# Eight full expert tiles taken from the first half of the tokens, the second half routed inside the expert loop

## The chip, the core and the metric

The kernel runs on one core of a Trainium2 chip. The metric is the device time of one execution in microseconds (us); the tables give the median of three runs. A profiled execution gives the rows that are quoted. The core's engines work side by side and meet only at semaphores: PE (TensorE, matrix products into PSUM), DVE (VectorE), ACT (ScalarE), POOL (GpSimd, which also issues gathers and scatters), and SP (SyncE, which issues most transfers here).

## The reference

One decoder layer over 2 x 1024 tokens of width 256, followed by a mixture of eight experts:

```python
x = _layernorm(x + attn(x))           # running sums of exp(keys) over the tokens
x = _layernorm(x + xattn(x, ctx))     # 16 heads, 77 context rows
# ffn:
logits = flat @ router_w.T + router_b
topk_vals, topk_idx = jax.lax.top_k(logits, 2)
topk_w = jax.nn.softmax(topk_vals, axis=-1)
for e in range(8):
    cw = jnp.sum(jnp.where(topk_idx == e, topk_w, 0.0), axis=-1)
    y = jax.nn.gelu(flat @ w1[e].T + b1[e], approximate=False)     # 256 -> 1024
    y = y @ w2[e].T + b2[e]                                        # 1024 -> 256
    out = out + y * cw[:, None]
out = _layernorm(out + hidden, ln_w, ln_b)
x = _layernorm(x + out)
```

Each token needs only its two chosen experts, so the kernel sorts the 4096 pairs of token and expert by expert and computes 128 pairs at a time.

## The kernel before

**Attention.** The 2048 tokens are 16 tiles of 128 (`TILES`), four to a chunk. After a start of its own, the cross attention runs in 64 steps (`attention_step(H)`, four steps to a token tile, each step four heads). The other stages of the layer for later tokens, and the norms, router logits and routing for earlier tokens, are hung on these steps by tables (`FIRST_STEPS`, `logits_step`, `RANKS_STEP`, `MARK_STEPS`). Every engine runs its own copy of the step loop, in the order written.

**Routing.** `SETS` splits the token tiles into 8, 4 and 4. For each set DVE finds the two best experts (`first_choice`, `second_choice`), PE counts with triangular matrices how many earlier tokens chose the same expert (`ranks`), DVE turns the ranks into places (`ranked`, `place`), and for each of the 2 x tiles pairs it writes two 128 x 128 indicator matrices (`mark`, L1211 and L1212), whose product on PE (`mark_pairs`, L1578) adds the token numbers into a table of 128 places by tile columns. Each expert owns 16 columns of places. Because the experts' tile counts are known only after the last set, DVE then makes the map (which expert and which column each of the 39 tiles has, L1269 to L1273), POOL turns it into integers (`map_tiles`), copies a tile's column of tokens and gathers the token rows (`load_tile`, L705 and L707). The first set is routed inside attention; the second partly and the third wholly after it.

**Expert loop.** 39 tiles (`SLOT_TILES`) of 128 pairs. On PE, tile t: `up(t)` (L1638, 32 products into `psum_a` or `psum_b`), `turn_rows(t+1)` (L1624, transposes of the gathered rows), `down(t-1)` (L1650, into `psum_v` or `psum_c`). ACT copies the transposed rows (`turned_rows`, L918), applies Gelu (`hidden`, L929) and prepares the weighed bias (`weighed_bias`, L941). DVE reads the gathered row's weight and row numbers (`indices`, L1294 to L1298), weighs the output (`weigh_output`, L1306), adds the input and the other expert's result if that came earlier (`sum_row`, L1317), and does the two norms (`inner_norm` L1325, `outer_norm` L1333). POOL does the powers for the norms (L723), gathers the earlier result of the same token from `weighed_outputs` (`load_base`, L714), gathers the rows of a tile five ahead, and scatters finished rows (L727). SP loads each tile's `w1` (1 MB, ring of three, `load_w1`) and stores the weighed outputs (`store_yw`).

**What ties them.** `up(t)` waits for the transposed rows, for `w1` and for Gelu of tile t-2; `down(t)` for Gelu of its tile and for `weigh_output(t-2)`; `weighed_bias(t)` for `sum_row(t-2)`; `load_base(t)` for the store of tile t-1; `load_w1(t)` for Gelu of tile t-3.

## Time and profile before

| | us |
|---|---|
| median of three runs (lowest, highest) | 557.19 (555.75, 559.47) |
| profiled execution, its time | 557.52 |
| its span in the trace | 555.7 |
| PE busy | 497.9 (90%), x3293 |
| DVE busy | 398.5 (72%), x1230 |
| ACT busy | 251.9 (45%), x838 |
| POOL busy | 259.9 (47%), x374 |

The span is cut into 40 equal slices of 13.9 us. Each digit is the busy share of a slice in tenths; PEclk is the granted clock of TensorE in tenths of full speed.

```profile
PE   6678999989999999418999999999999999999970
...
DVE  5768878676859986851568777776777778767744
ACT  3355667555765566103344344444443344344410
POOL 4543132221312300343367666675676767666643
PEclk9899999989999999857999999999999999999995
```

The chain that ended last, by engine:

```profile
PE 80%; DVE 10%; issue 2%; POOL 2%; DMA 2%; ACT 1%; SPq 1%; POOLq 0%; ACTq 0%; DVEq 0%
```

### The profile page before, as it was taken

To read this page: it belongs to the slowest core of one execution; us is meant where nothing else is said; L and a number is where in the kernel's file an instruction comes from. 1 tells how busy PE (TensorE), PEld (TensorE's weight loads), DVE (VectorE), ACT (ScalarE), POOL (GpSimd) and SP (SyncE) were. 2 spreads that over 40 slices of the span, in tenths; PEclk is the share of its full clock that TensorE was granted. 3 is DMA by queue.
4 is the path that set the end of the run, shared out by engine and by line. 5 is a ranking of instruction groups with operands and counts; after the bars stand their busy time and mean duration, and the time that the engine had idled before them with its cause. 6 is when DMAs were issued, how large, how long until landed. Compare 5 with 4: busy or idle time off the path is not lost.

```text
span 555.7 us, 10856 instructions
## 1 busy us (share of the span) xinstructions
PE 497.9 (90%) x3293; PEld 448.3 (81%) x3293; DVE 398.5 (72%) x1230; ACT 251.9 (45%) x838; POOL 259.9 (47%) x374
## 2 busy tenths in 40 slices
PE   6678999989999999418999999999999999999970
PEld 6567888878887877307999999999999999999960
DVE  5768878676859986851568777776777778767744
ACT  3355667555765566103344344444443344344410
POOL 4543132221312300343367666675676767666643
PEclk9899999989999999857999999999999999999995
DMA  7119991000000050027566555556566666666310
GB/s 226 13 38 335 338 321 50 11 9 11 11 9 11 11 120 21 24 90 280 189 202 211 197 203 196 194 203 216 209 220 216 222 211 221 214 217 211 97 46 16
DMA packets 43873, 81.14 MB, mean 146 GB/s; under 512 B 10768, under 2 KB 35610, under 8 KB 38696
## 3 DMA queue, kind: packets, MB, share of 16 engines
q1 hardware_dynamic: 36567, 67.36, 35.9%
q0 software_dynamic: 5616, 12.82, 7.6%
q8 instruction: 28, 0.46, 0.3%
q10 hardware_dynamic: 1632, 0.27, 0.3%
q14 instruction: 30, 0.24, 0.1%
HBM read 65.64 MB, written 17.63 MB: 150 GB/s over the span
## 4 chain that ended last, share of the span: by engine, by line
PE 80%; DVE 10%; issue 2%; POOL 2%; DMA 2%; ACT 1%; SPq 1%; POOLq 0%; ACTq 0%; DVEq 0%
PE psum_a L1638 13%; PE psum_b L1638 12%; PE psum_c L1650 12%; PE psum_v L1650 12%; PE psum_b L1377 7%; PE psum_v L1510 5%; PE psum_a L1476 5%; PE psum_m L1528 2%; PE psum_m L1377 2%; PE psum_c L1497 2%; PE psum_m L1624 2%; PE psum_a L1479 1%; DMA second_buffers<-in_x 1%; PE psum_c L1492 1%; PE psum_b L1384 1%
## 5 line engine op out<-in xcount | busy, mean ns | idle before, releaser
L929 ACT ACTIVATE front_then_w_ring<-psum_a,front_then_w_ring 128x128 f32<-128x128 f32 x160 | 45.7, 369 | 81.8 <-PE psum_a L1638 78.9
L1638 PEld LDWEIGHTS psum_a<-front_then_w_ring 128*128 128x128 f32 x640 | 76.8, 197 | 2.0 <-issue 1.0
L1638 PE MATMUL psum_a<-front_then_w_ring 128*128 128x128 f32 x640 | 77.0, 280 | 0.6 <-ACT front_then_w_ring L918 0.6
L929 ACT ACTIVATE front_then_w_ring<-psum_b,front_then_w_ring 128x128 f32<-128x128 f32 x152 | 43.5, 369 | 74.3 <-PE psum_b L1638 72.0
L823 ACT ACTIVATE work<-psum_a,score_max 128x77 f32<-128x77 f32 x256 | 62.4, 335 | 29.8 <-DVE score_max L1081 29.7
L1638 PEld LDWEIGHTS psum_b<-front_then_w_ring 128*128 128x128 f32 x608 | 70.8, 192 | 2.5 <-issue 1.6
L1650 PE MATMUL psum_v<-expert_w,front_then_w_ring 128*128 x320 | 72.4, 379 | 0.0
L1638 PE MATMUL psum_b<-front_then_w_ring 128*128 128x128 f32 x608 | 71.0, 275 | 1.4 <-ACT front_then_w_ring L918 1.4
L1650 PE MATMUL psum_c<-expert_w,front_then_w_ring 128*128 x304 | 68.8, 379 | 0.0
L1650 PEld LDWEIGHTS psum_v<-expert_w,front_then_w_ring 128*128 128x128 f32 x320 | 59.3, 190 | 7.3
L723 POOL TENSOR_TENSOR routing<-routing,minus_half 128x2 f32<-128x2 f32 x40 | 29.2, 729 | 74.0 <-DVE routing L1313 72.8
L1650 PEld LDWEIGHTS psum_c<-expert_w,front_then_w_ring 128*128 128x128 f32 x304 | 56.3, 190 | 6.9
L714 POOL DMA_INDIRECT work<-weighed_outputs,routing x39 | 46.4, 1190 | 16.8 <-issue 11.9
L1377 PE MATMUL psum_b<-front_then_w_ring,front_weights_then_tail 128*128 128x256 f32 (+1 forms) x216 | 48.6, 370 | 1.9 <-ACT front_then_w_ring L801 1.8
L1325 DVE SCALAR_TENSOR_TENSOR work<-work,routing,front_weights_then_tail 128x256 f32<-128x256 f32 x39 | 19.3, 496 | 37.0 <-POOL routing L723 37.0
L727 POOL DMA_INDIRECT out<-work,routing x39 | 40.2, 1030 | 12.1 <-issue 6.1
L1510 PEld LDWEIGHTS psum_v<-front_weights_then_tail,work 128*128 128x128 f32 x320 | 40.6, 192 | 5.1 <-issue 4.7
L1377 PEld LDWEIGHTS psum_b<-front_then_w_ring,front_weights_then_tail 128*128 128x128 f32 x216 | 37.7, 190 | 8.0 <-ACT front_then_w_ring L801 2.7
L707 POOL DMA_INDIRECT front_then_w_ring<-token_rows,routing x39 | 38.3, 983 | 11.1 <-POOL routing L705 10.8
L1510 PE MATMUL psum_v<-front_weights_then_tail,work 128*128 128x136 f32 x320 | 43.1, 282 | 0.0
L544 POOL TENSOR_TENSOR ln_rstd<-ln_veps,minus_half 128x2 f32<-128x2 f32 (+1 forms) x18 | 12.5, 696 | 59.3 <-DVE ln_veps L970 59.3
L567 POOL TENSOR_TENSOR routing<-routing,minus_half 128x1 f32<-128x1 f32 x16 | 10.4, 647 | 63.5 <-DVE routing L1046 63.5
(214 smaller groups left out, 927.0 us busy)
## 6 DMA issues: line engine op xcount, KB each, us to landing
front_then_w_ring<-in_w1b SPq DMA_DIRECT2D x39, 1028.0 KB
expert_w<-in_w SPq DMA_DIRECT2D x8, 1024.0 KB, 10.7
weighed_outputs<-routing SPq DMA_DIRECT2D x1, 4992.0 KB, 16.8
weighed_outputs<-work SPq DMA_DIRECT2D x39, 128.0 KB, 2.0
token_rows<-front_then_w_ring SPq DMA_DIRECT2D x16, 128.0 KB, 1.9
second_buffers<-in_x SPq DMA_DIRECT2D x4, 256.0 KB, 4.8
front_weights_then_tail<-in_b SPq DMA_DIRECT2D x1, 1024.0 KB, 8.3
front_then_w_ring<-in_x SPq DMA_DIRECT2D x3, 256.0 KB, 4.6
```

The lines of the kernel that those rows point to most:

```text
L707: pool.indirect_dma_start(xt[t % ROWS], None, rows_dram, bass.IndirectOffsetOnAxis(load_of[:, t % ROWS:t % ROWS + 1], 0)).then_inc(xt_in[t ...
L714: pool.indirect_dma_start(base[t % 3], None, yw_dram, bass.IndirectOffsetOnAxis(row_idx[:, t % IDX, 0:1], 0)).then_inc(base_in[t % 3], 16)
L723: pool.tensor_tensor(rstd[:, t % 4], veps[:, t % 2], mhalf[:, 0:2], ALU.pow).then_inc(rstd_out, 1)
L727: pool.indirect_dma_start(out, bass.IndirectOffsetOnAxis(row_idx[:, t % IDX, 1:2], 0), u_rows[t % 3], None, bounds_check=T - 1, oob_is_err ...
L823: last = act.activation(prob[:, u % RING_U, at_k:at_k + SC], pa[:, H % 2, g * SC:(g + 1) * SC], ACT.Exp, bias=smax[:, j % 2, head:head + 1])
L929: last = act.activation(hidT[t % 2][:, c, :], src[:, n, q * P:(q + 1) * P], ACT.Gelu, bias=bias[:, c:c + 1])
L1325: row(dve.scalar_tensor_tensor(u, base[t % 3], out_mv[:, t % 2, 0:1], lnw_s, ALU.subtract, ALU.mult))
L1377: last = pe.matmul(dst[:, c, :], w[:, k, c * P:(c + 1) * P], src[:, k, :], start=(k == 0), stop=(k == KD - 1))
L1476: pe.matmul(dst, qT[it % 2][:, half, j * P:(j + 1) * P], kbd[:, it // CPB, half, g * HG:(g + 1) * HG, :].rearrange("p h k -> p (h k)"), st ...
L1510: last = pe.matmul(pv[:, half * width:(half + 1) * width], probT[:, u % RING_U, c, :], vblk[:, t // (CPB * CT), half, c, :], start=(c == 0 ...
L1638: last = pe.matmul(dst[:, n, q * P:(q + 1) * P], w1[:, k, c * P:(c + 1) * P], xtT[t % 2][:, k, :], start=(k == 0), stop=(k == KD - 1))
L1650: last = pe.matmul(y_psum(t), hidT[t % 2][:, c, :], w2_v[:, bass.ds(e, 1), c, :].rearrange("p a d -> p (a d)"), start=(c == 0), stop=(c == ...
```

## The change

`SETS` becomes two halves of eight token tiles. Once the first half is routed, inside attention, a first map takes the first eight full tiles of 128 pairs that it holds (`first_map`, `FIRST = 8`); they are expert tiles 0 to 7, and they need no later token. Their pairs keep their places; pairs of the first half beyond them get 32768 added to their slot (`LATER`), so that of a token's two results the one computed later is known. The second half is routed after attention, while PE works on the first expert tiles: DVE does it between its work for tiles 0, 1 and 2, and a second map (`rest_map`, `later_map`) covers the other 31. PE starts tile 0 directly behind the last weighing of values, in halves (`up(t, n)`) put between the last tiles' projection, transposes and logits. The products for the first half's marks stand at step 56 of attention, those for the second half's behind `up(3)`.

Weighed outputs are stored by their slot (128 columns of 128 rows, `YW_COLS`), no longer by tile number, so DVE's correction of row numbers (three instructions of `indices`) goes, SP reads a column number before each store, and the array to be zeroed grows from 39 to 128 columns: 16 transfers of 1 MB, two behind each `store_x2` of tiles 2 to 9. The second half's token rows are zeroed too (`clear_rows`). The exponential of the routing moves from ACT to POOL, as a power. SP loads `w1` of tiles 0 to 2 behind `store_x2(10)`, inside attention, and POOL gathers the rows of tiles 0 to 3 in steps 58 and 62.

At the start of the kernel, the moments of x pieces 3 and 4 and the mask are moved behind the first key sums, and the warm-up products on PE go from 14 to 9. `slot(8)` and `slot(11)` change places.

```diff
-SETS = ((0, 2 * CT), (2 * CT, CT), (3 * CT, CT))
+SETS = ((0, TILES // 2), (TILES // 2, TILES // 2))
+LATER = 32768.0
-RANKS_STEP = (CHUNKS - 1) * STEPS + 3
+RANKS_STEP = (CHUNKS - 1) * STEPS + 1
...
+            def store_yw(t):
+                sp.wait_ge(yw_ready, t + 1)
+                col = nc.values_load(store_col_of[0:1, t:t + 1], engines=[mybir.EngineType.SP], min_val=0, max_val=YW_COLS - 1,
+                                     skip_runtime_bounds_check_because="the map keeps it below the number of columns")
+                sp.dma_start(yw_cols[bass.ds(col, 1)].rearrange("a p d -> p (a d)"), yw[t % 3]).then_inc(yw_out[t % 3], 16)
...
                 store_x2(t)
+                if t < 10:
+                    clear_yw(2 * t - 4)
+                    clear_yw(2 * t - 3)
+                if t == 10:
+                    store_ext(0)
+                    for n in range(RING3):
+                        load_w1(n)
...
             def mark_pairs(n):
-                    last = pe.matmul(pc[:, 0, 0:P], *marks_of(n, i), start=(done + i == 0), stop=(done + i == PAIRS - 1))
+                    last = pe.matmul(table_psum(n), *marks_of(n, i), start=(i == 0), stop=(i == SET_PAIRS[n] - 1))
...
-            for t in range(SLOT_TILES):
-                up(t)
+            for t in range(2, SLOT_TILES):
+                up(t, 0)
+                up(t, 1)
+                if t == 3:
+                    pe.wait_ge(placed, 3 * LAST + 1)
+                    mark_pairs(LAST)
                 if t + 1 < SLOT_TILES:
                     turn_rows(t + 1)
-                if t >= 1:
-                    down(t - 1)
+                if t - 1 == FIRST:
+                    pe.wait_ge(map_ready, 2 * MAPS)
+                down(t - 1)
```

The order on DVE behind attention is written out:

```diff
+            route_logits(TILES - 1)
+            first_choice(LAST)
+            second_choice(LAST)
+            indices(2)
+            weigh_output(0)
+            add_input(0)
+            rest_map()
+            ranked(LAST)
+            place(LAST)
+            for i in range(SET_PAIRS[LAST] // 2):
+                mark(LAST, i)
+            dve.wait_ge(ln_in, 2 * 16)
+            indices(3)
+            weigh_output(1)
+            add_input(1)
+            sum_row(0)
+            for i in range(SET_PAIRS[LAST] // 2, SET_PAIRS[LAST]):
+                mark(LAST, i)
+            later_map()
+            row(inner_norm(0))
+            sum_row(1)
+            dve.memset(token_of[:, P:COLS], 0.0)
+            dve.wait_ge(pos_mm, LAST + 1)
+            dve.tensor_tensor(token_of[:, 0:P], table_psum(LAST), first_token_of, ALU.add).then_inc(table_ready, 1)
+            for t in range(2, SLOT_TILES):
```

On PE, behind the last weighing of values (L1510), before the change. L1443 transposes a normed tile, L1564 to L1570 are rank counts, L1452 logits, L1528 the output projection, L1578 products of marks:

```order
L1443 MATMUL psum_b<-identity,front_then_w_ring 128x128 x2
L1520 MATMUL psum_m<-identity,work 128x128 x2
L1564 MATMUL psum_v<-routing 128x32
...
L1452 MATMUL psum_a<-front_weights_then_tail,work 128x8 x2
L1528 MATMUL psum_m<-front_weights_then_tail,work 128x256 x2
L1443 MATMUL psum_b<-identity,front_then_w_ring 128x128 x2
L1452 MATMUL psum_a<-front_weights_then_tail,work 128x8 x2
L1578 MATMUL psum_c<-front_then_w_ring 128x128 x16
...
L1578 MATMUL psum_c<-front_then_w_ring 128x128 x8
L1624 MATMUL psum_m<-identity,front_then_w_ring 128x128 x2
L1638 MATMUL psum_a<-front_then_w_ring 128x128 x16
```

The same place after it (L1677 is `turn_rows`, L1690 `up`, L1702 `down`):

```order
L1514 MATMUL psum_c<-identity,front_then_w_ring 128x128 x2
L1677 MATMUL psum_c<-identity,front_then_w_ring 128x128 x2
L1690 MATMUL psum_a<-front_then_w_ring 128x128 x8
L1589 MATMUL psum_m<-identity,work 128x128 x2
L1521 MATMUL psum_c<-front_weights_then_tail,work 128x8 x2
L1690 MATMUL psum_a<-front_then_w_ring 128x128 x8
L1677 MATMUL psum_c<-identity,front_then_w_ring 128x128 x2
L1597 MATMUL psum_m<-front_weights_then_tail,work 128x256 x2
L1514 MATMUL psum_c<-identity,front_then_w_ring 128x128 x2
L1690 MATMUL psum_b<-front_then_w_ring 128x128 x8
L1521 MATMUL psum_c<-front_weights_then_tail,work 128x8 x2
```

The first expert products moved ahead of everything but one transpose, and the marks moved away. On DVE, where the second half's places are made, after the change (L1344 is `weigh_output`, L1339 `add_input`, L1274 to L1282 `rest_map`, L1295 and L1296 marks):

```order
L1213 TENSOR_TENSOR routing<-routing 128x64
...
L1344 SCALAR_TENSOR_TENSOR work<-psum_v,routing,work 128x256
L1339 TENSOR_TENSOR work<-work,front_then_w_ring 128x256
L1274 TENSOR_SCALAR routing<-psum_c 128x8
...
L1224 TENSOR_TENSOR routing<-psum_c,routing 128x64
L1230 TENSOR_TENSOR routing<-routing 128x64
...
L1245 CAST routing<-routing 128x4x8
L1295 TENSOR_SCALAR second_buffers<-routing 128x128
L1296 TENSOR_SCALAR second_buffers<-routing 128x128
```

Tile 0's output is weighed between the choice and the places, and eight more pairs of marks stand behind tile 1's output and tile 0's sum.

## Rows read from the trace of the kernel before

**Rows 1.** window: length, busy PE PEld DVE ACT POOL, PEclk, DMA share, GB/s.
```profile
223.00:251.00 28.00, 9.07 (x70) 5.75 (x68) 19.85 (x98) 3.02 (x6) 11.67 (x29) 0.67 0.20 61
```

**Rows 2.** timeline of PE: start, duration, line, output and inputs, count.
```profile
221.73 1.32 PE L1510 MATMUL psum_v<-front_weights_then_tail,work 128*128 128x136 f32 x10
...
225.02 1.13 PE L1528 MATMUL psum_m<-front_weights_then_tail,work 128*128 128x256 f32 x4
...
251.60 6.09 PE L1638 MATMUL psum_a<-front_then_w_ring 128*128 128x128 f32 x32 [0.62 <-ACT front_then_w_ring L918]
...
534.46 3.62 PE L1650 MATMUL psum_v<-expert_w,front_then_w_ring 128*128 x16
```

**Rows 3.** timeline of PE in the settled expert loop.
```profile
397.02 3.73 PE L1638 MATMUL psum_a<-front_then_w_ring 128*128 128x128 f32 x32
...
400.59 0.38 PE L1624 MATMUL psum_m<-identity,front_then_w_ring 128*128 128x128 f32 x2
...
404.26 3.73 PE L1638 MATMUL psum_b<-front_then_w_ring 128*128 128x128 f32 x32
```

**Rows 4.** timeline of ACT between attention and the first tile.
```profile
235.54 1.28 ACT L944 ACT_TABLE_LOAD   x1
...
251.08 0.38 ACT L918 ACTIVATE front_then_w_ring<-psum_m 128x256 f32<-128x256 f32 x1 [14.25 <-PE psum_m L1624]
```

**Rows 5.** timeline of DVE, choice of experts for eight token tiles.
```profile
177.31 0.22 DVE L1149 TENSOR_REDUCE routing<-logits 128x8 f32<-128x64 f32 x1
...
178.60 0.23 DVE L1161 SCALAR_TENSOR_TENSOR routing<-routing,logits 128x64 f32<-128x64 f32 x1
```

**Rows 6.** timeline of DVE, placing eight token tiles, and marks.
```profile
190.93 0.22 DVE L1194 TENSOR_TENSOR routing<-routing 128x64 f32<-128x64 f32 x1
...
192.67 0.18 DVE L1203 CAST routing<-routing 128x32 f32<-128x32 int32 x1
...
198.20 0.28 DVE L1211 TENSOR_SCALAR front_then_w_ring<-routing 128x128 f16<-128x128 f32 x1
...
198.65 0.28 DVE L1211 TENSOR_SCALAR front_then_w_ring<-routing 128x128 f16<-128x128 f32 x1
```

**Rows 7.** timeline of DVE, last reduction of the tile map.
```profile
243.92 0.74 DVE L1273 TENSOR_REDUCE routing<-routing 128x80 f32<-128x560 f32 x1
```

**Rows 8.** timeline of DVE in the settled expert loop.
```profile
403.93 0.48 DVE L1325 SCALAR_TENSOR_TENSOR work<-work,routing,front_weights_then_tail 128x256 f32<-128x256 f32 x1 [0.85 <-POOL routing L723]
...
406.32 0.15 DVE L1294 COPY routing<-front_then_w_ring 128x1 f32 x1
...
407.55 0.47 DVE L1306 SCALAR_TENSOR_TENSOR work<-psum_c,routing,work 128x256 f32<-128x256 f32 x1
...
410.66 0.48 DVE L1325 SCALAR_TENSOR_TENSOR work<-work,routing,front_weights_then_tail 128x256 f32<-128x256 f32 x1 [0.85 <-POOL routing L723]
```

**Rows 9.** timeline of PE, then windows right behind it, columns as in 1.
```profile
117.96 0.44 PE L1492 MATMUL psum_c<-identity,work 128*128 128x128 f32 x2 [1.42 <-ACT work L823]
...
120.00:122.00 2.00, 2.00 (x11) 2.00 (x11) 1.97 (x4) 1.37 (x6) 1.27 (x1) 0.50 0.00 0
122.00:124.00 2.00, 2.00 (x10) 1.77 (x9) 2.00 (x4) 1.53 (x7) 0.73 (x1) 0.68 0.00 0
```

**Rows 10.** timeline of DVE and of SP's queue, first expert number to load.
```profile
237.25 0.15 DVE L1264 CAST routing<-routing 128x1 int32<-128x1 f32 x1
...
238.12 0.36 SPq L499 DMA_DIRECT2D front_then_w_ring<-in_w1b  x1
```

**Rows 11.** timeline of ACT and DVE near the start.
```profile
12.69 0.63 ACT L796 ACTIVATE front_then_w_ring<-psum_m,bka 128x128 f32<-128x128 f32 x2 [1.31 <-PE psum_m L1377]
...
15.08 0.85 DVE L995 TENSOR_TENSOR_SCAN front_then_w_ring<-one,carry,front_then_w_ring 128x128 f32<-128x128 f32 x2
```

**Rows 12.** timeline of PE, a late wait in attention.
```profile
218.26 0.44 PE L1492 MATMUL psum_c<-identity,work 128*128 128x128 f32 x2 [0.95 <-ACT work L823]
```

**Rows 13.** DMA issues: output and input, queue, count, size, us to landing.
```profile
weighed_outputs<-routing SPq DMA_DIRECT2D x1, 4992.0 KB, 16.8
```

More of the change, by code:

```diff
@@ L314, in decoder_layer @@
         slot_hl = tmp(TOPK, TILES)
+        later, low_i, low = tmp(TILES, E), tmp(TILES, dt=I32), tmp(TILES)
         higher = tmp(TILES, E)
@@ L590, in _ @@
             block_owners()
-            for p in range(2, 5):
-                input_rsqrt(p)
+            input_rsqrt(2)
             pool.wait_ge(made, MADE)
@@ L665, in rows_of_choice, with map_tiles, first_rows_ready, load_tile @@
                 pool.tensor_scalar(ext[:, ts, :, 2], higher[:, ts], float(NOWHERE), None, ALU.add).then_inc(ext_ready, 1)
+            def map_tiles(n):
+                ts = slice(0, FIRST) if n == 0 else slice(FIRST, FIRST + XS_TILES)
+                nt = FIRST if n == 0 else XS_TILES
+                pool.wait_ge(counted, n + 1)
+                pool.tensor_copy(expert_of[:, ts], passed[:, 0, 0:nt]).then_inc(map_ready, 1)
+                pool.tensor_copy(col_of[:, ts], colf[:, 0, 0:nt]).then_inc(map_ready, 1)
+                pool.tensor_copy(store_col_of[:, ts], colf[:, 1, 0:nt]).then_inc(map_ready, 1)
+                pool.wait_ge(map_ready, (n + 1) * MAPS)
+            def first_rows_ready():
+                pool.wait_ge(table_ready, 1)
+                for j in range(2):
+                    pool.wait_ge(x2_out[j], TILES // 4 * 16)
+                pool.wait_ge(rows_clear, 2 * 16)
+                pool.wait_ge(ext_out, 16)
+                pool.wait_ge(row0_out, 3 * 16)
+            def load_tile(t):
+                if t == FIRST:
+                    pool.wait_ge(table_ready, 2)
+                    for j in range(2):
+                        pool.wait_ge(x2_out[j], TILES // 2 * 16)
+                    pool.wait_ge(ext_out, 2 * 16)
+                col = nc.values_load(col_of[0:1, t:t + 1], engines=[mybir.EngineType.Pool], min_val=0, max_val=(P if t < FIRST else COLS) - 1,
+                                     skip_runtime_bounds_check_because="a tile's column is below the number of columns")
+                if t >= ROWS:
+                    pool.wait_ge(xl_ready, t - ROWS + 1)
+                    pool.wait_ge(var_ready, t - ROWS + 1)
+                pool.tensor_copy(load_of[:, t % ROWS:t % ROWS + 1], (first_token_of if t < FIRST else token_of)[:, bass.ds(col, 1)]).then_inc(load_ready, 1)
+                pool.wait_ge(load_ready, t + 1)
+                pool.indirect_dma_start(xt[t % ROWS], None, rows_dram,
+                                        bass.IndirectOffsetOnAxis(load_of[:, t % ROWS:t % ROWS + 1], 0)).then_inc(xt_in[t % ROWS], 16)
             for H in range(CHUNKS * STEPS):
@@ L924, in hidden @@
                     act.wait_ge(y_mm, t - 1)
[L925 to L931 removed]
+                act.wait_ge(h_mm, 2 * t + n + 1)
+                for c in range(n * KF // 2, (n + 1) * KF // 2):
+                    q = c - n * KF // 2
+                    last = act.activation(hidT[t % 2][:, c, :], src[:, n, q * P:(q + 1) * P], ACT.Gelu,
+                                          bias=bias[:, c:c + 1])
+                last.then_inc(hT_made, 1)
             def weighed_bias(t):
@@ L1194, in place @@
                 then(dve.tensor_tensor(slots[:, ts], slots[:, ts], both[:, ts], ALU.mult))
+                if n == 0:
+                    then(dve.tensor_tensor(later[:, ts], slots[:, ts], over_e(threshold, nt), ALU.is_ge))
+                    then(dve.scalar_tensor_tensor(slots[:, ts], later[:, ts], LATER, slots[:, ts], ALU.mult, ALU.add))
                 then(dve.tensor_reduce(slot_hl[:, 0, ts], slots[:, ts], AX.X, ALU.max))
```

462 lines of the change are left out of this document (228 added, 234 removed).

## Prediction

> **What bounds the kernel now.** I read the engine shares and the 40 slices first: PE is busy 90% of the span, and its row has one hole, in the 17th and 18th slice. The chain that ended last is 80% PE, and no other engine is above 10% of it. The windows show the hole: from 223 to 251 us PE is busy 9.07 of 28 us and DVE 19.85, at a mean granted clock of 0.67 [rows 1]. The timelines then give its parts. PE ends the last weighing of values at 221.73 + 1.32 = 223.05, the first `up` starts at 251.60, and the last `down` ends at 534.46 + 3.62 = 538.08 [rows 2]. Inside the loop an `up` starts every 404.26 - 397.02 = 7.24 us, 3.57 of them products of `up` [rows 3], and PE does not pause. So 39 tiles are 39 x 7.24 = 282.4 us of PE, and of the 315.0 us from 223.05 to 538.08, 32.6 are not expert work. The remaining 17.6 us are the tail. In the hole, DVE works through a serial chain: second set's places and marks, third set's choice, places and marks, map; after it come a gather, a transpose and a copy.
>
> **The change, part by part.** I count PE from the end of the last weighing of values (0) and let each engine wait where the code says.
>
> *PE before tile 2.* A transpose of the normed tile and the rows of tile 0 end at 0.4. ACT copies one (0.38), loads the Gelu table (1.28) and copies the other (0.38) [rows 4]; before, the table load lay in the hole. With 0.15 for two handovers `up(0,0)` starts at 2.4, a wait of about 2.0. The small groups that stay (three transposes, one turn of heads, three logits, one projection, the rank counts) are each no longer than the projection's 1.13 [rows 2]. By their passes I take 3.2 us in all; they can't be above the 9.07 that PE was busy in the hole. Two short waits, 0.6 for the last normed tile and 0.55 for the copy of tile 2's rows, are added. This puts the logits of the last tile at 13.0, the end of `down(0)` at 16.5, `up(2)` from 17.5 to 21.1, the end of `down(1)` at 24.8, and the end of `up(3)` at 28.4. There PE must have the sixteenth pair of marks.
>
> *DVE until then.* The choice for eight tiles costs (178.60 - 177.31)/5 = 0.258 per step [rows 5]; eleven steps and two unchained ones are 3.1, so it ends at 16.3. Tile 2's indices, and weighing and input of tile 0, are 1.3: 17.6. `rest_map` has six chained steps of 0.2 and three free ones of 0.1: 19.1. Ranks 0.26, places 192.67 + 0.18 - 190.93 = 1.92 and 0.2 for the two added instructions: 21.5. A pair of marks is 198.65 - 198.20 = 0.45 [rows 6]; eight are 3.6: 25.1. Tile 1's output and tile 0's sum are 2.4: 27.5. Eight more pairs: 31.1, and the last product ends at 31.5. PE waits 3.1 us. It is this wait, for DVE's marks, that takes the place of the old one.
>
> *PE's sum.* 282.4 + 3.2 + (2.0 + 0.6 + 0.55 + 3.1) = 291.9 in place of 315.0: **-23.1 us**.
>
> *After the marks.* The second map has 32 columns; its reduction over 560 elements took 0.74 before [rows 7], and it costs 1.8 in all. Two norms and a sum put the token table at about 36.4, and tile 2's output is weighed at 40, while `down(2)` ended at 35.2: DVE is 5 us late. `down(4)` is the first to ask for it, at 46. When DVE was behind, one round took 410.66 - 403.93 = 6.73 us, 407.55 - 406.32 = 1.23 of it `indices` [rows 8]. Three of its instructions go, which leaves about 0.3, so a round is 5.8 and DVE gains 1.4 on each tile of 7.24. The lag is gone after four tiles and PE does not see it. The table is wanted by tile 8's gather, which POOL issues three tiles later. This part costs 0 as long as DVE's round stays below 7.24; if it did not, the surplus would be paid on every tile.
>
> *The clock.* Behind a wait of 1.42 us that came after thin activity, the granted clock was 0.50 and 0.68 for two windows of 2 us; that is 2 x 0.50 + 2 x 0.32 = 1.6 us lost [rows 9]. There are two idle places now, 2.0 and 3.1 us. Bounds are 0 and 3.2; I take **+1.5**, one such fall. The Trainium skill ("TensorE: Matmul & The Clock Gate", What's actually happening) says that the throttled state is the default and that activity releases it. By this rule both idle places could end at half speed, and the sum would have 3.2 where mine has 1.5.
>
> *DVE beside POOL.* The second half's weights (two powers of eight columns) run on POOL during the places and marks. The instructions of `indices` in rows 8 lie beside POOL's gathers. I add **+0.6**, between 0 and 3, to the wait for marks, as a fifth of the 3 us of places and choice.
>
> *The store's register.* Each store of weighed outputs now reads a column number after its wait. The nearest rows: DVE finishes the first expert's number at 237.25 + 0.15, and SP's load that needs it issues at 238.12 [rows 10], 0.7 us with the read. In the loop it is hidden in DVE's waiting rounds; in the tail it is on the path once. Bounds 0 and 0.7; **+0.5**.
>
> *Attention.* At the start ACT ends the first exponentials at 12.69 + 0.63 = 13.3, but DVE begins to sum at 15.08, since moments and mask stand ahead [rows 11]. Moved behind, they bring up to 1.75; I take -1.7, since the rest of the start follows from this sum. Late in attention, DVE gets some 15 more short instructions at steps 49 and 50 (3.3 us at 0.2 to 0.26 each) and loses 13 of the middle set's choice at steps 60 and 61. The second has a wait of PE of 0.95 behind it [rows 12], which goes. The first comes in one block, between maxima for which ACT and PE wait, and the products of the first half's marks come in. I take +1.3, between -1 and +3.5. Together **-0.4**. A wrong guess here moves everything behind it one for one. The transfers that are moved into attention (zero fill, `w1` of three tiles, biases) are covered by it, see the rivals.
>
> *Sum.* -23.1 + 1.5 + 0.6 + 0.5 - 0.4 = -20.9 us against the profiled execution's 557.52 (span 555.7 and 1.8 around it), which is 0.33 above the median. So 557.19 - 20.9 = **536.3 us**.
>
> **The rivals.**
>
> *The marks come later (16 in 100).* The chain on DVE between last logits and last mark has some 70 instructions and passes through PE once. If each handover or POOL's use of the same memory adds a quarter to its 18 us, PE waits 4.5 more, and with both falls of the clock 6.2: 542.5. For it: `indices` took 1.23 us for five instructions of one column [rows 8]. Against it: the marks of rows 6 are taken in the crowded part of attention. The Trainium skill ("GPSIMD Engine Reference", Key points) says that POOL shares its SBUF interfaces with VectorE and contends with its two-port modes; by this rule the marks would stretch while POOL computes the weights.
>
> *More is won (12 in 100).* The clock does not fall and the late block in attention hides: 536.3 - 1.5 - 1.5 - 1 = 532.
>
> *The zero fill comes too late (3 in 100), the other side.* SP's queue must carry 18 MB of zeros ahead of tile 0's `w1`; before it was 5 MB, in 16.8 us [rows 13], or 304 GB/s. At this rate 18 MB are 59 us, spread over some 100 us of attention with idle transfer engines. At a third of it they would take 178 us, end at 270 and let `up(0)` start near 280: 28 us later than now, 585. It decides from the point where the fill ends behind 246, that is below about 115 GB/s. That is far from the row.
>
> *DVE's lag grows instead of shrinking (4 in 100).* If the round on DVE stays at 7.24 or above, because gathers of the earlier results come later with the longer store, PE pays for five tiles or more: about 550, still faster. If it lasts for all tiles at 7.8 the gain is gone.
>
> *The two halves overlap, but not for more than a few tiles (3 in 100),* that is, `map_ready` or the table for tile 8 is late. Its slack is some 13 us. It would give 545 to 557.
>
> **How the numbers follow.** My forecast gets 62 in 100, with 533.5 to 539.5 as its own range. The 8-in-10 range takes in most of the first two rivals: 531 to 543. One per cent is 5.6 us, about what can be told from no change. Faster by over 1%: forecast, marks and more won, most of the lag and overlap cases: 0.94. Within 1%: 0.02. Slower: the fill and the worst lag, 0.04.
>
> **What would show it.** Right if: the first `up` starts some 2.4 us behind the last weighing of values; in the timeline of PE the longest idle piece between 220 and 300 us is one of about 3 to 4 us just ahead of the transposes of tile 4, released by a mark on DVE; from then on an `up` starts every 7.24 us; the tail is 17 to 19 us. The granted clock near that wait tells the clock term, the start of the last weighing of values tells the attention term (223.05 now, 222.6 expected at its end). Wrong if DVE's weighing falls further behind `down` from tile to tile, if `up(0)` waits for a transfer, or if the last weighing of values ends behind 226.

## The result and the profile after

The changed kernel takes **543.36 us** (median of 4 runs, 541.52 to 543.66), the kernel before, on the same chip, 558.33 (4 runs, 555.75 to 559.65). The ratio is 0.9731, with a 95% interval of 0.9685 to 0.9776. So the change gives 15.0 us, where 20.9 were predicted; 543.36 lies just above the range of 531 to 543, and above the forecast's own range. The profiled executions, 557.52 before and 543.59 after, have spans of 555.7 and 541.9 us: 13.8 us apart. In the run *The start* below, one of four executions took 753.09 us at a mean granted clock of 0.65, and the time given there is the median of the other three.

The page of the changed kernel, engine shares and three rows of the 40 slices:

```profile
PE 496.7 (92%) x3283; PEld 446.7 (82%) x3283; DVE 374.2 (69%) x1111; ACT 250.0 (46%) x835; POOL 259.8 (48%) x370
...
PE   6778999989999869988999999999999999999960
...
DVE  3777978868768977528877656766676666766644
...
PEclk9999999999999979999999999999999999999995
```

Of the deep hole that PE had in the 17th and 18th slice, two digits of 8 are left, in the 18th and 19th. There is a new hole ahead of it, in the 15th (190 to 203 us), and there the clock is low too. The timeline of PE there and behind it (start, duration, line, what; in brackets the idle time before a group and what released it; L1579 weighs values, L1690 is `up`, L1646 a mark product, L1702 `down`):

```profile
189.61 0.60 PE L1453 MATMUL psum_b<-identity,second_buffers 128*128 128x128 f32 x4
195.00 0.69 PE L1561 MATMUL psum_c<-identity,work 128*128 128x128 f32 x2 [4.79 <-ACT work L864]
...
197.62 2.24 PE L1579 MATMUL psum_v<-front_weights_then_tail,work 128*128 128x136 f32 x10
```

```profile
228.05 1.32 PE L1579 MATMUL psum_v<-front_weights_then_tail,work 128*128 128x136 f32 x10
...
231.85 2.02 PE L1690 MATMUL psum_a<-front_then_w_ring 128*128 128x128 f32 x16 [2.04 <-ACT front_then_w_ring L944]
...
247.56 0.19 PE L1634 MATMUL psum_c<-routing 128*128 128x72 f16 x1 [1.05 <-DVE routing L1213]
...
259.66 1.01 PE L1646 MATMUL psum_c<-second_buffers 128*128 128x128 f16 x11
...
262.76 0.39 PE L1677 MATMUL psum_m<-identity,front_then_w_ring 128*128 128x128 f32 x2
...
266.83 3.73 PE L1690 MATMUL psum_a<-front_then_w_ring 128*128 128x128 f32 x32
...
274.08 3.73 PE L1690 MATMUL psum_b<-front_then_w_ring 128*128 128x128 f32 x32
```

```profile
520.19 3.62 PE L1702 MATMUL psum_v<-expert_w,front_then_w_ring 128*128 x16
```

These rows split the difference of the spans into three parts, with the end of the last weighing of values as the first cut and the end of the last `down` as the second:

| part | before [rows 2] | after | difference | predicted |
|---|---|---|---|---|
| start to end of last weighing | 223.05 | 228.05 + 1.32 = 229.37 | **+6.3** | -0.4 |
| from there to end of last `down` | 315.03 | 520.19 + 3.62 - 229.37 = 294.44 | -20.6 | -23.1 + 1.5 + 0.6 = -21.0 |
| tail | 17.6 | 18.1 | +0.5 | +0.5 |

The part the change is about came out as forecast. What was lost is in attention, which ends 6.3 us later instead of 0.4 earlier.

Where in attention? I compared the start of each of the 32 weighings of values in the two traces. Counted from 0, weighing 0 is 0.8 us later than before (42.76 against 41.96), 1 to 12 are 0.54 later, and from 13 on they are 0.5 earlier; that step is the clock, which fell at 120 us before [rows 9] and not in this execution. Nothing moves until weighing 22 (181.28 against 181.78). Then 6.8 us are lost. The windows, first from weighing 13 to 22, where most of the zero fill runs, then from 22 to the end of the last (start:end, length, busy time of PE, PEld, DVE, ACT, POOL with instructions, granted clock, DMA share, GB/s), before:

```profile
127.49:181.78 54.29, 53.39 (x340) 45.64 (x339) 42.18 (x115) 32.64 (x112) 11.88 (x15) 1.00 0.04 13
181.78:223.05 41.27, 38.37 (x270) 32.65 (x268) 33.13 (x128) 26.03 (x99) 7.08 (x14) 1.00 0.20 48
```

and after:

```profile
127.01:181.28 54.27, 53.38 (x339) 45.64 (x338) 42.15 (x115) 32.55 (x112) 11.84 (x15) 1.00 0.51 168
181.28:229.37 48.09, 41.48 (x287) 35.46 (x286) 33.81 (x132) 25.80 (x97) 13.99 (x26) 0.93 0.48 163
```

In the first pair the transfer engines went from 4% to 51% busy and the stretch kept its length (54.29, 54.27). So the zero fill costs nothing here. The Trainium skill ("Trainium Architecture — The Big Picture", What this means for kernel authors) says that engine lanes and DMA ports of SBUF can't contend with each other; these rows agree. The weights of the first three expert tiles lie elsewhere: SP issues them from 197.0 to 199.8 us, in the second stretch and behind PE's long wait in it. No run takes them out; but every wait of PE over 0.3 us from 181 to 229 is released by ACT, none by a transfer. In the second pair PE is idle 6.6 us in place of 2.9 and busy 3.1 us more, at a lower mean clock.

DVE shows what PE waited for. These are its maxima of steps 49 and 50 (L1121) and the first and last instruction that routing puts between them:

```profile
186.17 0.48 DVE L1121 TENSOR_REDUCE score_max<-psum_a 128x4 f32<-128x308 f32 x1
...
188.42 0.20 DVE L1262 TENSOR_SCALAR routing<-routing 128x8 int32<-128x8 int32 x1
...
193.25 0.17 DVE L1245 CAST routing<-routing 128x32 f32<-128x32 int32 x1
193.46 0.48 DVE L1121 TENSOR_REDUCE score_max<-psum_a 128x4 f32<-128x308 f32 x1
```

`first_map` and `place(0)` are 5.0 us in one piece, and they stand behind step 49's own work of 2.3 us (a residual with its moments and a norm). So 7.29 us lie between two maxima. The exponentials wait for the second, PE waits for them, and behind the wait PE runs at half clock: the weighing at 197.62 takes 2.24 us, not 1.32.

### The profile page after: what moved, and what is told of

The parts are those of the page before. It is cut to its first block, busy times and chain, and to the rows that moved or that the text cites. A ratio compares the mean times of both kernels' runs of the same rounds, so it can differ in the third digit from the quotient of the medians.

```text
span 541.9 us, 10883 instructions
## 1 busy us (share of the span) xinstructions
PE 496.7 (92%) x3283; PEld 446.7 (82%) x3283; DVE 374.2 (69%) x1111; ACT 250.0 (46%) x835; POOL 259.8 (48%) x370
## 4 chain that ended last, share of the span: by engine, by line
PE 80%; DVE 11%; issue 3%; POOL 3%; ACT 2%; POOLq 0%; DMA 0%; DVEq 0%; SPq 0%; ACTq 0%
PE psum_a L1690 13%; PE psum_b L1690 12%; PE psum_v L1702 12%; PE psum_c L1702 11%; PE psum_b L1446 8%; PE psum_v L1579 6%; PE psum_a L1545 5%; PE psum_m L1597 2%; PE psum_m L1446 2%; PE psum_c L1566 2%; PE psum_m L1677 1%; PE psum_a L1548 1%; PE psum_c L1561 1%; PE psum_b L1453 1%; DVE front_then_w_ring L1050 1%
## 5 line engine op out<-in xcount | busy, mean ns | idle before, releaser
L1690 PEld LDWEIGHTS psum_a<-front_then_w_ring 128*128 128x128 f32 x640 | 74.5, 192 | 3.9 <-issue 3.0
L1690 PE MATMUL psum_a<-front_then_w_ring 128*128 128x128 f32 x640 | 75.1, 275 | 2.6 <-ACT front_then_w_ring L944 2.0
L1702 PE MATMUL psum_v<-expert_w,front_then_w_ring 128*128 x320 | 72.6, 380 | 0.1
L1690 PEld LDWEIGHTS psum_b<-front_then_w_ring 128*128 128x128 f32 x608 | 70.9, 192 | 0.9
L1690 PE MATMUL psum_b<-front_then_w_ring 128*128 128x128 f32 x608 | 71.1, 275 | 0.0
L1702 PE MATMUL psum_c<-expert_w,front_then_w_ring 128*128 x304 | 68.8, 379 | 0.0
L1702 PEld LDWEIGHTS psum_v<-expert_w,front_then_w_ring 128*128 128x128 f32 x320 | 59.3, 190 | 7.6 <-issue 0.4
L1702 PEld LDWEIGHTS psum_c<-expert_w,front_then_w_ring 128*128 128x128 f32 x304 | 56.3, 190 | 6.9
L1579 PEld LDWEIGHTS psum_v<-front_weights_then_tail,work 128*128 128x128 f32 x320 | 41.1, 194 | 5.1 <-issue 4.9
L1355 DVE TENSOR_TENSOR work<-work 128x256 f32<-128x256 f32 x39 | 16.6, 425 | 40.3 <-DMA work<-weighed_outputs,routing 34.2
L1579 PE MATMUL psum_v<-front_weights_then_tail,work 128*128 128x136 f32 x320 | 43.2, 283 | 0.0
```

The source lines that it names most:

```text
L1579: last = pe.matmul(pv[:, half * width:(half + 1) * width], probT[:, u % RING_U, c, :], vblk[:, t // (CPB * CT), half, c, :], start=(c == 0 ...
L1690: last = pe.matmul(dst[:, n, q * P:(q + 1) * P], w1[:, k, c * P:(c + 1) * P], xtT[t % 2][:, k, :], start=(k == 0), stop=(k == KD - 1))
L1702: last = pe.matmul(y_psum(t), hidT[t % 2][:, c, :], w2_v[:, bass.ds(e, 1), c, :].rearrange("p a d -> p (a d)"), start=(c == 0), stop=(c == ...
```

## The experiments

Executions of one kernel lie 1.3 to 6.5 us apart. An edit worth 1 to 3 us is therefore read from its stretch of the trace, and the time is quoted beside it.

**Two blocks in place of one.** The map stays at step 49, the places go to step 50, the marks start a step later.

```diff
                 if H == RANKS_STEP:
                     first_map()
+                if H == RANKS_STEP + 1:
                     place(0)
-            MARK_STEPS = tuple(RANKS_STEP + n for n in (1, 2, 4, 5, 6))
-            MARKS = ((0, 3), (3, 8), (8, 11), (11, 13), (13, 16))
+            MARK_STEPS = tuple(RANKS_STEP + n for n in (2, 3, 4, 5, 6))
+            MARKS = ((0, 5), (5, 8), (8, 11), (11, 13), (13, 16))
```

> Only the place of the first half's DVE work in attention changes: the map of the first eight tiles stays in step 49, places go to step 50, and the marks start one step later. No instruction is added or removed. Theory A, the block: in the changed kernel DVE runs 5.0 us of routing between the maxima of steps 49 and 50 (188.42 to 193.42), PE is idle for 4.79 us, and the granted clock of 0.5 to 0.66 behind it costs another 1.9 or so. Cut in two pieces of 2.4 and 2.7 us, each is hidden for the most part: longest idle piece of PE between 185 and 205 under 1.5 us, the last weighing of values ends near 223 in place of 229.4, and the time is 537 to 538.5 in place of 543.4. Theory B, the amount: DVE has some 3 us more work in these steps and is full in any case, so the stall is only spread: 541.5 to 543.5. Theory C, the transfers moved into attention (zero fill, rows, expert weights) cause the loss: 543.4, no change.

Measured: 542.46 us, ratio 0.9723 (0.9690 to 0.9756). PE and its window from weighing 22 to the last:

```profile
194.33 0.44 PE L1562 MATMUL psum_c<-identity,work 128*128 128x128 f32 x2 [2.07 <-ACT work L864]
...
195.71 2.43 PE L1580 MATMUL psum_v<-front_weights_then_tail,work 128*128 128x136 f32 x10
```

```profile
183.33:228.23 44.90, 40.99 (x287) 35.17 (x286) 33.61 (x132) 25.86 (x97) 14.21 (x26) 0.96 0.51 175
```

The stretch falls from 48.09 to 44.90, the wait from 4.79 to 2.07. The two maxima stand 4.57 us apart here (188.22 and 192.79). Taking 2.72 us out from between them took 2.72 us from the wait: PE had 2.50 us in hand (7.29 - 4.79 = 4.57 - 2.07), and at this place what DVE puts between the two maxima beyond that is paid one for one. It is not so everywhere: the next two maxima of this run stand 4.02 us apart (192.79 and 196.81), and behind them PE has no wait over 0.3 us. Before the change the places stood at step 51, a light one, with maxima at 190.54 and 192.97, 2.43 apart, and PE did not wait. But the gain is 3.2 of the 6.8 us only, so theory A, as I put it, does not hold in full, and the time does not show even that (0.9723, against 0.9731 for the changed kernel, with intervals that overlap; 537 to 538.5 us was expected). In the profiled execution the start was 1.0 us later (first weighing at 43.76), and the clock fell at 121 us as well, which put weighing 13 another 1.0 us later.

**Dealt out over nine steps.**

```diff
-                if H == RANKS_STEP:
-                    first_map()
+                if H == RANKS_STEP + 1:
+                    thresholds()
+                if H == RANKS_STEP + 2:
                     place(0)
-                if H == RANKS_STEP + 9:
+                if H == RANKS_STEP + 3:
+                    map_of(tbend, spare, FIRST, 0.0)
+                if H == RANKS_STEP + 10:
...
+            MARK_STEPS = tuple(RANKS_STEP + n for n in (3, 4, 5, 6, 7, 8))
+            MARKS = ((0, 2), (2, 4), (4, 6), (6, 10), (10, 14), (14, 16))
```

`thresholds` is `first_map` without the call of `map_of`; the products of the marks, the table and the first gathers each move one or two steps.

> In the run with two blocks PE was still idle for 2.07 us in one piece, DVE was busy without a pause from 188 to 201 us, and the last weighing of values ended 1.1 us earlier only, 2.3 of its 3.2 us gain being hidden by more half clock elsewhere. Here the same DVE work is dealt out over nine steps: thresholds at step 50, places at 51, the map at 52, marks at 52 to 57, their products at 58, the token table at 59, the first gathers at 60. Theory A1, what a step can take: PE runs dry when DVE has more than about 3 us between two maxima. Then no idle piece of PE over 1.3 us stands between 180 and 222, the distance from weighing 22 of the values (181.28 in the changed kernel) to the end of the last one is 41 to 42.5 us in place of 48.1 (before: 41.3), and the time is 536 to 538. Theory B, the amount: as DVE is full there, the distance stays above 44 (two blocks: 44.9) and the time above 540. A rival loss: tile 0's gather, two steps later, comes too late and the first up waits for a transfer.

Measured: 542.09 us, ratio 0.9764 (0.9704 to 0.9825). The window and all waits of PE over 0.3 us between 196.5 and 215:

```profile
182.90:228.02 45.12, 40.31 (x287) 33.25 (x286) 33.29 (x132) 26.11 (x97) 14.15 (x26) 1.00 0.50 174
```

```profile
196.72 0.55 PE L1569 MATMUL psum_c<-identity,work 128*128 128x128 f32 x3 [0.46 <-ACT work L865]
...
199.66 0.44 PE L1517 MATMUL psum_c<-identity,front_then_w_ring 128*128 128x128 f32 x2 [0.88 <-ACT work L865]
...
204.58 0.44 PE L1564 MATMUL psum_c<-identity,work 128*128 128x128 f32 x2 [1.29 <-ACT work L865]
...
213.98 0.44 PE L1564 MATMUL psum_c<-identity,work 128*128 128x128 f32 x2 [1.23 <-ACT work L865]
```

The long wait is gone and the clock stays up, yet the stretch is as long as with two blocks. Theory B has the numbers right (over 44, over 540), but its cause, the amount of DVE work, is not shown: in this stretch DVE is busy 33.29 us, and it was busy 33.13 us before the change. From 196 to 214 DVE does not pause, and small waits of PE take the place of the long one. Just ahead of that, DVE stands still:

```profile
193.54 0.41 DVE L1095 TENSOR_SCALAR front_then_w_ring<-front_then_w_ring,routing 128x256 f32<-128x256 f32 x1 [2.17 <-POOL routing L589]
```

It waits for POOL's power of the norm (L589, at 192.95). POOL has the routing's weights ahead of it, whose exponential the change moved to POOL: they take it from 187.78 to 192.99. Before the change the same power ran at 188.12, ahead of them. No run puts it back there. The two maxima around this pause are 5.13 us apart (190.05 and 195.18), and PE waits 0.46 us behind them, so here it has more in hand than 2.50. The rival, a gather of tile 0 that comes too late, is out: the first `up` starts 2.48 us behind the last weighing, as in the changed kernel.

Against before, 3.85 us remain: PE is busy 1.94 us more, of which the 16 mark products, now inside attention, are 0.9 to 1.1 (they start at 214.62 in the changed kernel, what follows starts at 215.52), and the rest is idle. So of the 6.8 us some 3 are the block (wait and half clock), and some 3.8 remain in this order of the work.

**The start.** 14 warm-up products again, and POOL and DVE take the first residual's norm ahead of the next input piece.

```diff
-WARM = 9
+WARM = 14
...
             weigh_keys(0, 0)
+            rsqrt(LN2, 0)
             input_rsqrt(3)
             keys_table(0, 1)
-            rsqrt(LN2, 0)
...
-            input_moments(3)
             x1_moments(0)
+            input_moments(3)
```

> Only the first 25 us change: 14 warm-up products in place of 9 (as before the change), POOL's power for the first residual norm ahead of the second input norm's and of a keys table, and on DVE the first residual's moments ahead of the fourth piece's input moments. Theory A, the clock at the start: with nine products the first key projections ran at 2.08 us each in place of 1.16 (half clock), and the gain of an earlier sum was lost to that and then to POOL's queue. Then the key projections take 1.16 again, the first normalise of the residual starts near 22.3 in place of 23.8, the first weighing of values starts at 40.5 to 41.5 in place of 42.76, and the time falls by 1.2 to 2.3 us: 541 to 542.2. Theory B, the start is bound by something else (the input's transfers): the first weighing stays at 42.5 to 42.8 and the time within 0.4 of 543.4.

Measured: 541.62 us, ratio 0.9711 (0.9678 to 0.9745). The first weighing starts at 41.17, 1.6 us earlier than in the changed kernel. The gain does not reach the end of attention in the profiled execution (229.43), since the clock fell at 119 us (1.0) and for longer behind the stall of 4.80 (0.6).

**The warm-up alone.**

> The changed kernel with 14 warm-up products in place of 9, nothing else. It splits the gain at the start (first weighing of values at 41.17, 39.6 and 39.7 with both edits, against 40.8 to 44.5, mean 43.4, in six kernels with 9 products and the old order). If the half clock behind the short warm-up is what costs, the key projections take 1.16 us each and the first weighing starts near 41 to 41.5; the order on POOL and DVE then gives the last 1 us. If the order does it all, the first weighing starts at 42.5 or later, since the longer warm-up also puts the first transpose 1.3 us later. Time 541.5 to 543.

Measured: 544.00 us, ratio 0.9781 (0.9742 to 0.9820); its four executions are 540.93, 541.73, 546.27 and 546.88, so the time settles nothing. The profile does. The first key products of the changed kernel, and of this one:

```profile
8.41 2.08 PE L1446 MATMUL psum_m<-front_then_w_ring,front_weights_then_tail 128*128 128x128 f32 x8 [0.96 <-ACT front_then_w_ring L820]
11.21 2.08 PE L1446 MATMUL psum_m<-front_then_w_ring,front_weights_then_tail 128*128 128x128 f32 x8 [0.71 <-ACT front_then_w_ring L829]
```

```profile
8.74 1.16 PE L1446 MATMUL psum_m<-front_then_w_ring,front_weights_then_tail 128*128 128x128 f32 x8 [0.96 <-ACT front_then_w_ring L820]
10.85 1.16 PE L1446 MATMUL psum_m<-front_then_w_ring,front_weights_then_tail 128*128 128x128 f32 x8 [0.94 <-ACT front_then_w_ring L829]
```

With nine products the two key groups run at half clock, 2.08 us and not 1.16. The first weighing starts at 40.11 with 14, against 42.76. The other kernels say the same, if they are read at the second weighing. The first can mislead: in five kernels the key products ahead of it ran at half clock and put it 1.7 us later, and PE's next wait took that up. So it is at 41.37 in the kernel with all edits, not at 39.7 as the expectation has it, and at 45.66 and 46.02 in two kernels with 9 products. Of six with 9 products, one or both of the first key groups were slow in five, and the second weighing started between 51.88 and 53.63; in the sixth both took 1.16, and it started at 49.91. Of six with 14, the second group was slow in one (1.90 us, second weighing at 50.30); the others started between 48.32 and 49.24. Before the change it was 51.34. So it is the clock at the start, and the shorter warm-up undid the gain of the earlier key sum; what spreads the five slow starts over 1.75 us stays open. The order on POOL and DVE is worth 0.4 to 0.9 us beside it (48.32 to 48.80 against 49.24).

**Mark products one tile later.** `if t == 3:` ahead of `mark_pairs(LAST)` becomes `if t == 4:`.

> Only the place of the second half's sixteen mark products on PE changes: behind up(4) in place of behind up(3). Theory A, the wait for marks is worth what PE idles there: up(4) starts near 263.7 in place of 266.83, no wait for marks remains (0.9 us of products stays), DVE's token table is about 0.5 us later, which nothing waits for, and the time is 2.0 to 2.5 us lower: 541.1. Theory B, DVE is 4 to 5 us behind at that place and the wait only moves to a down that asks for an earlier weighed output: within 0.5 of 543.4.

Measured: 540.35 us, ratio 0.9691 (0.9662 to 0.9719).

```profile
261.73 3.62 PE L1702 MATMUL psum_v<-expert_w,front_then_w_ring 128*128 x16
265.19 3.73 PE L1690 MATMUL psum_a<-front_then_w_ring 128*128 128x128 f32 x32
268.76 1.06 PE L1646 MATMUL psum_c<-second_buffers 128*128 128x128 f16 x16
269.65 0.39 PE L1677 MATMUL psum_m<-identity,front_then_w_ring 128*128 128x128 f32 x2
```

The products run without a wait in 0.9 us. From the end of the last weighing (231.27) to the end of the span it takes 309.83, in place of 541.9 - 229.37 = 312.53: 2.7 us less. The wait does not come back at a later `down`, which was theory B. The wait that I took for unavoidable was a matter of where PE asks; only the 0.9 us of the products stay.

**Gelu table behind the first copy**, together with the edit above: on ACT, `turned_rows(0)` stands ahead of `preload_act_table`.

> The kernel with the marks' products behind up(4), and besides ACT loads the Gelu table behind the copy of tile 0's rows, not ahead of it. If PE's wait ahead of the first up is that load, the first up starts 1.2 to 1.3 us earlier (1.2 behind the last weighing of values in place of 2.48), the load lies beside it, and the time from the last weighing to the end is 1.0 to 1.3 us below the 309.8 of the marks-later kernel: 308.6. Rival: DVE's choice sets the end of this stretch, PE only waits longer ahead of the ranks (over 2 us in place of 1.05), and nothing is won.

Measured: 539.51 us, ratio 0.9695 (0.9661 to 0.9729).

```profile
226.12 1.32 PE L1579 MATMUL psum_v<-front_weights_then_tail,work 128*128 128x136 f32 x10
...
228.50 2.02 PE L1690 MATMUL psum_a<-front_then_w_ring 128*128 128x128 f32 x16 [0.62 <-ACT front_then_w_ring L944]
```

The first `up` starts 1.06 us behind the last weighing, not 2.48, and the end comes after 308.46 us, 1.4 less than 309.83. The rival is out.

**The bias sum later.** On POOL, `add_bias(0)` moves behind `weigh(1)` and `rows_of_choice(1)`.

> Only POOL's sum of tile 0's input and the last norm's bias moves, from ahead of the second half's weights to behind its rows. Theory: two instructions of DVE's choice took 0.85 and 0.57 us where their twins took 0.30 and 0.17, just while that sum (0.76 us, two operands in SBUF) ran on POOL; they make DVE late by 1.0 us, and PE waits 1.05 us for it ahead of the ranks and later for the marks. Then both instructions return to about 0.3 and 0.2, PE's wait ahead of the ranks falls below 0.3, up(2) and up(4) start 0.9 to 1.1 us earlier against the last weighing of values, and the time is 0.5 to 1.1 lower than 543.4. Rival: the slow-down comes from POOL's power instructions or from the gathers' transfers, which now stand there; then the two are slow as before or others are.

Measured: 545.05 us, ratio 0.9772 (0.9727 to 0.9817). Two steps of DVE's choice and POOL beside them, in the changed kernel:

```profile
245.83 0.85 DVE L1193 TENSOR_TENSOR routing<-routing 128x64 f32<-128x64 f32 x1
246.71 0.57 DVE L1219 TENSOR_TENSOR routing<-routing 128x8 f32<-128x8 f32 x1
```

```profile
246.49 0.76 POOL L759 TENSOR_TENSOR work<-front_then_w_ring,front_weights_then_tail 128x256 f32<-128x256 f32 x1
```

and with the sum moved:

```profile
249.24 0.23 DVE L1193 TENSOR_TENSOR routing<-routing 128x64 f32<-128x64 f32 x1
249.50 0.17 DVE L1219 TENSOR_TENSOR routing<-routing 128x8 f32<-128x8 f32 x1
```

The two fall to 0.23 and 0.17, PE no longer waits ahead of the ranks for more than 0.1 us, and `up(2)` starts 0.8 us earlier against the last weighing (+18.57, not +19.40). So the sum is the cause: POOL's gather lies beside both instructions in this run too (from 248.92) and does not slow them, and the powers come behind them in both kernels. It is the run that shows it, more than the overlap in the rows, where the first instruction starts 0.66 us ahead of the sum. Only half of the gain reaches `up(4)`, which starts 0.35 us earlier (+37.11 and +37.46). The sum slows DVE in its new place as well, where it lies beside a mark, which took 0.27 or 0.28 us before:

```profile
256.96 0.74 DVE L1295 TENSOR_SCALAR second_buffers<-routing 128x128 f16<-128x128 f32 x1
```

```profile
256.80 0.83 POOL L759 TENSOR_TENSOR work<-front_then_w_ring,front_weights_then_tail 128x256 f32<-128x256 f32 x1
```

The first mark starts 0.83 us earlier against the last weighing of values, and what follows the eighth pair 0.36 us earlier. The time of 545.05 us does not show the gain at all (0.5 to 1.1 less than 543.4 was expected); the profiled execution, 546.64 us, had the late start (44.51) and both falls of the clock. The Trainium skill ("GPSIMD Engine Reference", Specifications) names VectorE instructions with two SBUF inputs among those that contend with POOL for SBUF; the trace agrees for these two, both of this form.

**Together.** First the edits with two blocks, the start and the marks:

> The three edits of this call together. If they act in different places they add: by the theories A 5.5 + 1.7 + 2.2 = 9.4 us less than the changed kernel, 534 us, some 24 us below the kernel before. If the gains share a cause (all DVE's lateness), the sum is clearly smaller: 537 to 539.

Measured: 535.17 us, ratio 0.9598 (0.9571 to 0.9625), close to the 534 of edits that add. Then spread work, start, marks, table and bias sum:

> All edits so far together: spread DVE work, start order and 14 warm-up products, marks' products behind up(4), Gelu table later, bias sum later. If they add, the time is 535.2 (three edits) less 1.5 to 3 for the remaining stall in attention, less 1.2 for the table, less up to 1 for the bias sum: 530 to 532.5. If DVE's amount of work bounds the late part of attention or the stretch around the ranks, it stays at 533.5 or above.

Measured: 534.15 us, ratio 0.9594 (0.9576 to 0.9612), above the 530 to 532.5 of edits that add. Part of this is the spread work: from weighing 22 to the last it needs 45.08 us, and the three edits with two blocks need 44.01. Last, the same with two blocks in place of the spread, and that kernel once more:

> As the kernel with all edits, but with DVE's late work in attention in two blocks in place of spread. From weighing 22 of the values to the end of the last one the two-block kernels needed 44.90 (with half clock behind the stall) and 44.01 us (without), the spread ones 45.12 and 45.08. Theory: the amount of DVE work decides there and not its place; the two forms differ by the clock only. Then this kernel needs 44.0 when the clock stays up and 45.5 when it falls, and its time lies within 1.2 us of that of the spread kernel in this call. Against it: if the stall of 2.07 us brings the clock down in most executions, it is 1 to 1.5 us slower.

> The kernel with all edits and the spread work once more, for the comparison with the two-block form on one chip and for a narrower interval: 533 to 535, ratio to the kernel before 0.957 to 0.961.

Measured: 533.57 us, ratio 0.9572 (0.9554 to 0.9590), and 533.75 us, ratio 0.9588 (0.9570 to 0.9606). The two-block kernel's windows from weighing 22 to the last and from there to the end:

```profile
177.81:221.81 44.00, 39.53 (x287) 33.51 (x286) 33.38 (x132) 25.98 (x97) 14.22 (x26) 1.00 0.53 178
221.81:529.40 307.59, 287.56 (x2001) 270.15 (x1998) 204.10 (x632) 119.16 (x395) 193.35 (x242) 0.98 0.55 182
```

The times of the two forms lie within 0.2 us, as expected. That does not show that the amount of work decides and not its place: from weighing 22 to the last the spread form takes 45.08 us here too, 1.08 more than 44.00, with the same instructions and a granted clock of 1.00 in both. Both forms beat the kernel before by some 23.8 us and the changed kernel by some 9. Behind attention the edits add: the last stretch is 307.59, against 312.53 in the changed kernel, and 2.7 + 1.4 + 0.4 = 4.5 of these 4.9 us are known one by one.

## Why the prediction was wrong, point by point

**The failed step is attention, -0.4 us, measured +6.3.** It was two terms, which came to +7.3 together. The missing fall of the clock at 120 us took 1.0 off, and that was luck.

*The start, -1.7, measured +0.5 to +0.8.* I counted the earlier key sum, and it came: DVE starts it at 14.12, in place of 15.08 [rows 11], though ACT's exponentials ended later (14.0, in place of 13.32). I left out a line of the same diff, the warm-up from 14 to 9, which the description of the change tells of. With 14 the first weighing starts at 40.11, 1.85 us earlier than before. So the term had the right size for a start at full clock.

*The late block, +1.3 (-1 to +3.5), measured +6.8.* The count of added instructions was right (3.3 us), its reading was not. First, I priced what was added and not what was moved: `place(0)`, 2.7 us here, went from a light step, where it had cost nothing, to step 49, which has 2.3 us of its own. What counts is the distance between the two maxima, 7.29 us, against the 2.50 that PE has in hand at this place. Second, the half clock behind a wait of 4.8 us was not in this term. Third, the mark products are 0.9 us of PE in a stretch where PE waits for nothing else; I mentioned them and gave them no number. The best form tried leaves +2.7 (44.00 against 41.27), with a wait of 2.07 us still in it. Whether another order comes down to +1.3 stays open.

The text said that it would be wrong if the last weighing ended behind 226. It ended at 229.37.

**PE's sum, -23.1 and +2.1 for clock and DVE: right, partly by compensation.** 294.44 us were measured, 294.0 forecast.

- First `up` 2.48 us behind the last weighing (2.4).
- Marks: PE is held from 259.66 to 262.76, 3.1 us (3.1). It is held there product by product, 0.22 us at a time at the end, as DVE's marks come in; the text expected the longest idle piece here, but without a break that is the 2.04 ahead of the first `up`. The last product is at +33.4, not +31.5: the choice took 4.2 us, not 3.1 (243.19 to 247.4), mostly by POOL's sum beside it.
- PE came to `up(3)` 1.9 us late as well (end +30.3, not +28.4), by the 1.05 wait ahead of the ranks and small pieces. Hence the same wait.
- Clock, +1.5: 0 in this execution, the granted clock is 1.00 from 229.37 to 275. The three-edit kernel shows the other outcome. Behind the same wait of 2.04 us its first half of `up` takes 2.77 us:

```profile
224.62 2.77 PE L1691 MATMUL psum_a<-front_then_w_ring 128*128 128x128 f32 x16 [2.04 <-ACT front_then_w_ring L944]
```

  and its last stretch is 311.56 us, 1.7 above 309.83. The term was of the right size for one in eight executions. The row it came from was read too high: the fall near 120 us, taken as 1.6 us, put the weighings behind it 1.0 us later.

**DVE's lag, 0: right.** It weighs tile 2's output 4.1 us behind `down(2)`, tile 3's 3.0 and tile 4's 2.1 (271.11, 277.27 and 283.55 against ends at 267.00, 274.24 and 281.49). It gains 1.0 a tile, not 1.4, and PE never waits; from `up(4)` on the period is 7.24 (266.83, 274.08).

**The store's register, +0.5: right in size.** The tail is 18.1 us, it was 17.6; no run takes the read out to show that it is the cause.

**The rivals.** The late marks had the right mechanism, POOL beside DVE, at 1.0 us in place of 4.5. The zero fill came in time. The rival that happened was not on the list: a block of DVE work in attention itself. It lay inside a term with a range, and the range ended at +3.5.

## What to carry to other kernels

When serial work is put between two instructions that another engine waits for, price the distance between them, what already stands there included, against what the waiting engine has in hand; at the place measured here the surplus was paid in full. What it has in hand differs from place to place (2.50 us at one, at least 4.0 at two others), so read it from the trace for the very place. Moving work counts like adding it. And read every line of a diff that touches the start: a few warm-up products decide whether the first real ones run at 1.2 or at 2.4 GHz.

## What the hardware showed that I had not expected

The clock's falls depend on more than the length of a wait. All six profiled kernels with the 4.8 us wait in attention fell to 0.50 behind it. Behind 2.07 us one of three did, behind 2.04 us ahead of the first `up` one of eight, and behind the wait of 1.42 us near 117 us four of thirteen, the kernel before among them [rows 9]. Near 35 us it fell behind a wait of 0.94 or 0.95 us in three of five kernels and of 1.42 us in two of seven (16 key products in 4.56 or 4.57 us, not 2.89), and did not fall behind 1.85 us in the kernel before. One such fall costs 1 to 1.7 us, unless a later wait of PE takes it up as near 35 us, so two executions of one kernel differ by 2 us and more for this alone. The Trainium skill ("TensorE: Matmul & The Clock Gate", What's actually happening) has the throttled state as the default that activity releases; that agrees with the start, where a key group was slow in five of six changed kernels with nine products and in one of six with 14, and it does not foretell which of the short waits ends at half speed.
